# Fetching edge scores in groups of eight: GpSimd waits for VectorE's maxima once in eight fetches instead of at every fetch

## The reference, cut to what matters

```
z  = jnp.einsum('ni,hif->nhf', h, W)              # 2500 x 4 heads x 256
el = jnp.einsum('nhf,hf->nh', z, a_l)             # a score of each node as a source
er = jnp.einsum('nhf,hf->nh', z, a_r)             # and as a target
e  = jax.nn.leaky_relu(el[src] + er[dst], 0.2)
m  = jax.ops.segment_max(e, dst, num_segments=N)  # largest score of each target node
ex = jnp.exp(e - m[dst])
```

## Time and profile before

| | |
|---|---|
| three runs, us | 3145.21, 3158.06, 3157.28 (median 3157.28) |
| span of the profiled execution, us | 3172.0 |
| mean granted TensorE clock, of full speed | 0.943 |
| first to last fetch of edge scores (line 1132), us | 1244.36 to 1823.15 |
| first to last maximum (line 1379), us | 1304.97 to 1865.86 |

### The profile page before, as it was taken

One profiled execution on the slowest core, in us unless ns is written; L12 is line 12 of the kernel. 1 busy time (PEld: TensorE's weight loads), 2 busy tenths in 40 slices (PEclk: granted clock), 3 DMA queues, 4 the chain that ended last, 5 costly groups with the idle time before them and its releaser, 6 DMA issues. The chain is left out here.

```text
span 3172.0 us, 49827 instructions
## 1 busy us (share of the span) xinstructions
PE 2750.2 (87%) x13389; PEld 2152.8 (68%) x13389; DVE 2445.8 (77%) x5315; ACT 1667.2 (53%) x3377; POOL 1658.5 (52%) x1473
## 2 busy tenths in 40 slices
PE   4999969999997998477877789999999789499997
PEld 3788734444445776355656568888888678388886
DVE  8656769999997676356666589999999986677875
ACT  3555623333334525122222259999999754366664
POOL 1788757766663562555555525555555332034333
PEclk9999989999998999789898899999999889599999
DMA  5433489999991031001010138888888854588886
GB/s 182 115 94 101 159 304 342 340 345 342 345 335 50 7 135 54 13 17 22 16 22 15 22 140 309 304 311 306 309 308 309 257 192 162 203 228 230 230 235 160
DMA packets 197470, 600.30 MB, mean 189 GB/s; under 512 B 42763, under 2 KB 52354, under 8 KB 196174
## 3 DMA queue, kind: packets, MB, share of 16 engines
q0 software_dynamic: 135040, 429.23, 42.5%
q1 hardware_dynamic: 62286, 169.29, 15.3%
HBM read 513.25 MB, written 84.95 MB: 189 GB/s over the span
## 5 line engine op out<-in xcount | busy, mean ns | idle before, releaser
L663 POOL DMA_INDIRECT g_rows<-z_rows,edge_src x704 | 731.6, 1039 | 513.4 <-PE g_totals L1550 227.7
L1132 POOL DMA_INDIRECT shared<-el_rows,edge_src x352 | 337.1, 958 | 317.3 <-DVE t_largest L1379 164.1
L1512 PE MATMUL g_sums<-g_rows,g_share 128*128 128x256 f32 x1760 | 446.0, 388 | 2.9 <-issue 1.6
L704 ACT ACTIVATE g_scaled_hi<-g_rows,edge_weight_sorted 128x1024 fp32r<-128x1024 f32 x176 | 202.6, 1151 | 361.7 <-DMA g_rows<-z_rows,edge_src 346.7
L1379 DVE TENSOR_REDUCE t_largest<-t_masked 128x4 f32<-128x512 f32 x352 | 234.4, 685 | 160.9 <-PE t_masked L1218 112.3
L718 PE MATMUL g_sums<-g_rows,g_share 128*128 128x512 f32 x704 | 333.4, 596 | 21.1 <-DMA g_rows<-z_rows,edge_src 21.1
L1512 PEld LDWEIGHTS g_sums<-g_rows,g_share 128*128 128x128 f32 x1760 | 308.8, 191 | 37.0 <-issue 2.4
L331 POOL DMA_INDIRECT edge_list<-payload,row_i x196 | 259.9, 1326 | 125.8 <-issue 116.5
L739 DVE SCALAR_TENSOR_TENSOR g_scaled_lo<-g_rows,edge_weight_sorted,g_scaled_hi 128x1024 fp32r<-128x1024 f32 x176 | 225.6, 1282 | 54.1 <-ACT g_scaled_hi L704 39.2
L1216 PE MATMUL t_masked<-t_never,t_apart 128*128 128x512 f32 x352 | 158.1, 449 | 109.0 <-DVE t_largest L1379 88.3
L1485 ACT ACTIVATE g_scaled_hi<-g_rows,g_factor 128x256 fp32r<-128x256 f32 x528 | 227.9, 494 | 15.1 <-DMA g_rows<-z_rows,edge_src 9.7
(11 more groups left out here) (407 smaller groups left out, 7553.3 us busy)
## 6 DMA issues: line engine op xcount, KB each, us to landing
e_raw<-in_L_ffn_rw_dram SPq DMA_DIRECT2D x28, 1024.0 KB
g_rows<-z_rows,edge_src POOLq DMA_INDIRECT x704
g_place_of<-place_rows SPq DMA_DIRECT2D x44, 256.0 KB
z_rows<-z_zout SPq DMA_DIRECT2D x20, 512.0 KB
x_rows<-x_all SPq DMA_DIRECT2D x20, 512.0 KB
z_rows<-t_zout SPq DMA_DIRECT2D x20, 512.0 KB
s_x<-x_rows SPq DMA_DIRECT2D x20, 512.0 KB
xn_rows<-s_rows SPq DMA_DIRECT2D x10, 1024.0 KB
```

What stands on the lines that cost most here:

```text
L663: pool.indirect_dma_start(out=r.rows[:, slot, :], out_offset=None, in_=table, in_offset=bass.IndirectOffsetOnAxis(ap=g.src[:, i * GT + q:i ...
L1132: q.indirect_dma_start(out=g.edge_el[:, n, :], out_offset=None, in_=g.el, in_offset=bass.IndirectOffsetOnAxis(ap=g.src[:, n:n + 1], axis=0 ...
L1512: t.matmul(sums[:, it.buf(2), h // 2, h % 2 * HF:(h % 2 + 1) * HF], share[:, it.buf(2), n, :], r.rows[:, it.buf(4) * GT + q, h * HF:(h + 1 ...
```

## The change

GpSimd's wait moves out of the single fetch. At every eighth fetch (n = 0, 8, 16, ...) it waits for as many maxima as the last of the next eight would need plus one, and then issues the eight with no wait between them. All other engines' programs are the same, and all transfers.

```diff
+EL_BURST = 8
...
             for n in range(NE):
-                at_least(pool, taken, n - EL_LEAD)
+                if n % EL_BURST == 0:
+                    at_least(pool, taken, n + EL_BURST - EL_LEAD)
                 q.indirect_dma_start(
                     out=g.edge_el[:, n, :], out_offset=None, in_=g.el,
                     in_offset=bass.IndirectOffsetOnAxis(ap=g.src[:, n:n + 1], axis=0),
                 ).then_inc(el_in[BATCH_OF[n]], 16)
```

## The result

The changed kernel takes 3186.30 us (median of 4 runs, 3173.23 to 3189.44) against 3151.39 us (4 runs, 3145.21 to 3158.06) of the kernel before on the same chip: ratio 1.010, 95% interval 1.008 to 1.013. It is slower by 1%; the prediction said 0.8% faster.

A forecast was written before the change was run, and what follows sets the result against it. The prediction took late TensorE completions, caused by contention with GpSimd's fetches, as the bound. Tile chain -23 and start -1.3 summed to -24 us from 3157, giving 3133 us, 0.8% faster; 8-in-10 range 3100 to 3180.

The forecast's parts named there:

- The bound: In the stage's stretch of fetches, GpSimd's fetches contend with TensorE's completions, which come late; costs up to 178 us.
- VectorE did not wait for the data: At `parts(b)`, fetched scores arrive in time: needed 28 us after the last fetch's gate, which begins 8.8 us later.
- The landing: Time for a batch's last fetch to arrive before `parts(b)`: about 2.0 us fixed cost, with 9.7 us left.
- a passed wait costs nothing: In GpSimd's fetch series, 272 waits fewer save 0: the gap between fetches is 0.30 us either way.
- The test on line 1379: VectorE's line takes 627 to 693 ns throughout, so the trace shows no SBUF contention with GpSimd on the maxima.
- Each fetch series is now exactly eight: In the stretch of fetches, odd single fetches go away; a series of eight alone gives 1.47 us a chunk.
- I take half as spared: In the tile chain, half of VectorE's 16 waits of 2.9 us for ScalarE's cast go away: -23 us.
- The start: First series has 40 fetches instead of 41, so TensorE's completions there come sooner: 1.3 us less.
- The shift: GpSimd is quiet seven chunks more at the stage's start and seven fewer at its end: 4 us each way, cancelling.
- The rival "slower": Series of eight run on when completions turn late, each ending 1.26 us later: +49, net +25, 3182 us; chance 0.23.
- The rule that I had weighed: For GpSimd's fetches, a series of eight costs no more than eight single ones, so the time stays 3157 us.

The follow-up runs named there:

- e5: Kernel before with a 128x448 GpSimd clearing behind each fetch, fetches 1.605 us apart: 3124.62 against 3149.87 us, ratio 0.992.
- e9: Changed kernel (groups of eight) with a 128x448 GpSimd clearing behind every fetch: 3126.34 against 3153.67 us of the kernel before, ratio 0.992.
- e3: Changed kernel with groups of sixteen fetches instead of eight: 3279.71 against 3163.41 us of the kernel before, ratio 1.037.
- e10: Changed kernel with three 128x448 GpSimd clearings behind every eighth fetch, forcing a pause: 3134.55 against 3153.67 us of the kernel before, ratio 0.995.
- e8: Kernel before with no wait for maxima, all 352 fetches in a row: 3418.74 against 3149.87 us, ratio 1.086.

## Why the prediction was wrong

**The bound: right.** Fetches in a row make TensorE's completions late, and this sets the pace: 304 fetches left out give 126 us back, 352 without a wait cost 269 us. I put the most that contention could cost at 178 us, and 126 came back. That VectorE did not wait for the data held too: neither trace, before or after, has such a wait at `parts(b)`. The landing, for which I had no row, is 2.2 to 2.5 us from the start of the fetch in e5, near the 2.0 that I had taken. (One count was off by one, without effect: in the kernel before the last fetch of a batch is let go at 16b - 25, so 18 maxima ahead and not 17.) That a passed wait costs nothing is what e9 against e5 shows. The test on line 1379 said less than I made of it: the line reads PSUM and writes only four numbers a partition to SBUF, so it says little on contention for SBUF.

**"Each fetch series is now exactly eight", at 1.47 us a chunk: the step that failed.** The condition that I wrote down, that the next series can begin when eight more maxima are taken, is right. I read one case of it, in which maxima had come at 1.05 us and stopped after six, and made its outcome the rule for all series. Where they come faster, eight are in before the eighth fetch is out (x8 ahead of 1400.20 above; the last is done 7.0 us after the series began, and GpSimd needs 10.1), the next gate is open, and the series is sixteen. My own figures had it: 8 x 1.05 is 8.4 us, below the floor of 10.1 that I had written down beside it. The four sixteens last 20.2 us and a pause of 10.0, 10.7, 7.7 and 11.8 us each: 121 us for 64 chunks, where 1.47 gives 94. Nor was 1.47 the pace of the eights: with eight of them followed by 5.4 to 9.0 us they come to 1.64.

What the sixteens cost against the kernel before can be read chunk by chunk in the two traces. These 64 chunks took 103.9 us before and 120.9 after, 17.0 more. The 200 other chunks between the 41st and the 305th maximum took 336.4 before and 329.6 after, 6.8 less. The opening up to the 41st maximum took 5.3 less, and what follows the 305th maximum 8.6 more (54.2, now 62.8). Together these are the 13.6 us of the stage, and the sixteens are the largest part. In e3, all sixteens, every group is followed by such a pause. With series kept at eight, e10 is 0.5% faster than its kernel before, where 0.8% was forecast; but 13.0 us of what it gains on the changed kernel lie in the opening, which I had not counted on.

**"I take half as spared", -23 us: wrong in sum.** VectorE waits 3.3 us for a cast against 2.9, 12 times against 15, with three more of 9.1 us in all under another name: 48 us in all against 44, so nothing is gained. It splits as above. The three casts inside sixteens wait 24.5 us, where the same three waited 13.3 before; the twelve others wait 23.7 us, where they waited 30.4. Outside the sixteens some of the forecast's saving is there, inside them it is lost again. A late stretch lasts until GpSimd stops, and I had changed what makes it stop.

**The start, -1.3 us:** right in sign, it was -2.9 us to the first copy of rows in these two executions. **The shift, 4 us each way:** it did not cancel. From the 1st to the 41st maximum the changed kernel is 2.6 us shorter, behind the 305th 8.6 us longer; e10 has the same end (62.2 us), and no run tells why it costs more than the 4 us.

**The rival "slower", +25 us, 3182:** its first sentence, that GpSimd's stop at a missing maximum protects TensorE, is what e8 and e3 show, and its time was nearly met. Its price was worked out from another detail, one fetch more in every series; what happened is eight more in a few. The rule that I had weighed, from the Trainium skill, "DMA: Bandwidth & Descriptors", section "Anatomy of one DMA — SWDGE (gpsimd) path", that many descriptors can be emitted before an incremental cost shows, would have left the time at 3157. It speaks of the transfer's own cost, and GpSimd's 0.95 us for a fetch does stay the same along a series of sixteen. As a rule for the kernel's time it fails here, since others pay: between groups of 8 and of 16 the ratio goes from 1.010 to 1.037.

**Open:** through what the fetches delay TensorE's completions. The runs fit a backlog that grows when fetches stand close (1.26 and 1.34 us apart, a little still at 1.445) and drains when they stand 1.605 us apart or pause, but that is argued from the distances and no run looks inside. Open too is the end of the stage, and whether the short pauses of the changed kernel have a share in the 19.6 us that e10 saves in the chunks of the sixteens.

## What to carry to other kernels

A wait that looks like idle time of a feeder can be the brake that keeps it from hurting others: before thinning waits out, ask what stops the engine when its consumers fall behind, and whether the next gate can already be open when a group ends (group size times the consumer's quickest pace, against the group's own length). Where a small transfer delays others by its rhythm, set the distance between transfers rather than the place of the wait, and try several: 1.34, 1.445 and 1.605 us gave 0.4, 1.5 and 0.8%, with the best short of where the fetches become the bound, although completions are then not yet all prompt. When a spacing helps less than hoped, look who now waits for the spaced transfers before blaming the old contention.

## What the runs showed of the hardware

- 352 indirect fetches of 128 rows of 16 bytes, 1.26 us apart, let VectorE see one mask product in 11.1 or 14.1 us by turns in most of that stretch (1350.43, 1361.56, 1375.63 above), two in 25.2 us or 20 fetches. With 350 of them 1.605 us apart no maximum waits more than 3.1 us for its mask.
- With fetches 1.605 us apart VectorE starts on a batch's scores 2.2 to 2.5 us after the batch's last fetch began, in 18 of the 21 batches for which it waits (e5).
- These tiny transfers cost more than GpSimd's 0.95 us for each shows: without 304 of them the program is 126 us shorter, 0.41 us a fetch, although GpSimd's own time is not the bound.
- The granted clock of TensorE was 0.52 of full speed, near its lower level of 1.2 GHz, in the 403 us in which it mostly stood still, and 0.96 behind them.
